# A graph network on one core: at most two row gathers in flight, counted by two alternating semaphores

## The chip, the cores and the metric

The kernel runs on one core of one Trainium2 chip. The metric is the device time in microseconds (us) of one launch, the median of several runs. TensorE multiplies matrices, VectorE and ScalarE do elementwise work, GpSimd issues the gathers (DMAs that fetch rows by a list of indices), SyncE issues the plain loads and stores.

## The reference

Four graph layers over the same 206,250 directed edges, sorted by target, and 6,250 nodes of 128 features. Layer 0 is a message network, layers 1 to 3 are attention layers with 4, 4 and 8 heads. Between them stand residual additions and layer norms. Cut to what matters:

```python
# layer 0
msg_in = concatenate([x[src], x[tgt], edge_features], axis=-1)
messages = relu(msg_in @ W1 + b1) @ W2 + b2
agg = segment_sum(messages, tgt, num_segments=n) / counts
# layers 1 to 3, with small differences
h = (x @ W).reshape(n, HEADS, C)
e = leaky_relu(a_s[src] + a_d[dst], NEG_SLOPE)
p = exp(e - segment_max(e, dst)[dst])
out = segment_sum(h[src] * (p / segment_sum(p, dst)[dst])[:, :, None], dst)
```

What counts here is `x[src]` and `h[src]`: for every edge a row of a table in device memory is fetched by the number of the edge's source node.

## The kernel before, in words

The edges are cut into tiles of 128 and chunks of K = 13 tiles; there are CH = 124 chunks, PAIRS = 62 pairs of them. Each layer runs over all the chunks and then does its work on the nodes (a node stage), which writes the table of rows for the next layer. A table row has 128 numbers (512 bytes) in layer 0 and 144 (576 bytes) in layers 1 to 3.

The gathered rows of a chunk stand in `G`, which has two buffers, b = 0 and 1, for even and odd chunks. GpSimd's function `edges` (L562 to L570) waits until the chunk's indices are loaded and, past the first two chunks of a layer, until the messages of the chunk before last have been made from the same buffer. It then issues 13 gathers of 128 rows each, with no wait between them. All 13 count on one semaphore `gathered[l][b]`, of which there is one for each layer and buffer; a DMA adds 16 to it when it has landed. So 4 x 124 x 13 = 6448 gathers are issued, in order, from one queue.

Who waits for `gathered`: SyncE at L436 ahead of loading the indices two chunks on (behind it are queued the loads of edge features in layer 0 and of marks and joins in the others); ScalarE at L980 in layers 1 to 3 ahead of its copy of the source scores out of `G` (the copy helper's line is L925); VectorE at L1272 in layer 0 ahead of the four additions at L1276. The messages of a chunk are ready after L1276 and L1281 in layer 0, and after the multiplication at L1356 in the others. TensorE turns the membership tiles (L703), multiplies and adds up the messages by target (L713), and does the small products of the attention. Work on chunk c+1 is interleaved with that on chunk c by an order written out by hand on each engine.

Of the kernel before, what the change touches and what calls it, by code (L numbers as in the profile page):

```python
# [5 lines left out]
def gnn_program(nc, A, out):  # L6
# [20 lines left out]
    K = A["src"].shape[2]  # L27
    CH = A["src"].shape[0]
    TILES = K * CH
    PAIRS = CH // 2  # L30
# [26 lines left out]
    with ctx:  # L57
        def sb(name, shape, dt=fp32):
            return ctx.enter_context(nc.sbuf_tensor(name, shape, dt))
# [3 lines left out]
        def sem(name, counter=False):  # L63
            s = ctx.enter_context(nc.semaphore(name))
            if counter:
                counters.append(s)
            return s
# [23 lines left out]
        idx = sb("idx", [P, 2, K], i32)  # L91
# [146 lines left out]
        x_loaded = [sem(f"features_loaded{k}") for k in range(4)]  # L238
        row0_stored = [sem(f"first_rows_stored{k}") for k in range(4)]
        gather_paced = sem("gather_paced")  # L240
        built = sem("constants_built")
        cleared = sem("weights_cleared")
        targets_in = sem("targets_loaded")
# [8 lines left out]
        adz_clear = sem("padded_scores_cleared")  # L252


        gathered = [[sem(f"gathered_l{l}_{b}") for b in range(2)] for l in range(4)]
        idx_loaded = [sem(f"indices_loaded{b}") for b in range(2)]
        ef_loaded = [sem(f"edge_features_loaded{b}") for b in range(2)]
        marks_loaded = [sem(f"marks_loaded{b}") for b in range(2)]
# [87 lines left out]
        def past(l, c):  # L346

            return 2 + CH * l + c

        def gpast(l, c):  # L350

            return 2 + CH * (l - 1) + c
# [3 lines left out]
        def _(sp):  # L356
# [15 lines left out]
            def load_indices(l, c, b):  # L372
                sp.dma_start(idx[:, b, :], A["src"][bass.ds(c, 1), :, :]
                             .rearrange("o p k -> p (o k)")).then_inc(idx_loaded[b], 16)

            def load_edge_features(c, b):
                t0 = c * (K * P)
                sp.dma_start(ef[0:ED, b, :], A["edge_attr_64"][:, bass.ds(t0, EF)]).then_inc(ef_loaded[b], 16)
                sp.dma_start(ef[ED:2 * ED, b, 0:K * P - EF],
                             A["edge_attr_64"][:, bass.ds(t0 + EF, K * P - EF)]).then_inc(ef_loaded[b], 16)  # L380
# [47 lines left out]
            def load_marks(l, c, b):  # L428
                sp.dma_start(marks[0:JH, b, :], marks_all[bass.ds(c * K, K), :].unsqueeze(0)
                             .to_broadcast([H, K, 3 * P])).then_inc(marks_loaded[b], 16)  # L430
                sp.dma_start(join[0:1, b, :], joins_all[bass.ds(c, 1), :]).then_inc(marks_loaded[b], 16)

            def edges(l, c, b, h, last=False):
                if last:
                    return
                sp.wait_ge(gathered[l][b], 16 * K * (h + 1))  # L436
                load_indices(l, c + 2, b)
                if l == 0:
                    sp.wait_ge(pre_ready[3], past(0, c))
                    load_edge_features(c + 2, b)  # L440
                else:
                    sp.wait_ge(max_ready, gpast(l, c))
                    sp.wait_ge(maxf_ready, gpast(l, c))
                    sp.wait_ge(carry_ready, gpast(l, c))
                    load_marks(l, c + 2, b)
# [73 lines left out]
            for s in range(NS):  # L519
                left = min(BLK, N - s * BLK)  # L520
                sp.wait_ge(n_xnew, OUTER + s + 1)
                r = (INNER + s) % 3
# [11 lines left out]
        def _(pool):  # L534
# [27 lines left out]
            def edges(l, c, b, h, early=False):  # L562
                pool.wait_ge(idx_loaded[b], 16 * (PAIRS * l + h + 1))
                if not early:
                    pool.wait_ge(messages, past(l, c - 2))
                pool.sem_inc(gather_paced, 1)
                for t in range(K):
                    nc.gpsimd.indirect_dma_start(  # L568
                        G[:, b, t, 0:rows[l].shape[1]], None, rows[l],
                        bass.IndirectOffsetOnAxis(idx[:, b, t:t + 1], 0)).then_inc(gathered[l][b], 16)  # L570

            def base_rows(l, s):

# [349 lines left out]
        def _(act):  # L923
            def copy(dst, src):
                return nc.scalar.activation(dst, src, ACT.Copy)  # L925
# [18 lines left out]
            def keep_turned(l, c, j):  # L944
                act.wait_ge(turned[j], past(l, c))
                if l == 0:
                    act.wait_ge(pre_ready[j], past(l, c - 1))
                k0, k1 = BATCH[j]
                copy(membT[:, k0:k1, :], ps_mT[j % 2][:, 0:(k1 - k0) * P].rearrange("p (k n) -> p k n", k=k1 - k0)
                     ).then_inc(turned_kept[j], 1)  # L950
# [26 lines left out]
                        keep_turned(0, c + 1, j)  # L977

            def attention(l, c, b, h, ahead=True):
                act.wait_ge(gathered[l][b], 16 * K * (h + 1))  # L980
                copy(sflat[:, :].rearrange("p (h k) -> p h k", h=H),
                     G[:, b, :, MW:SW].rearrange("p k h -> p h k")).then_inc(sc_kept, 1)
                if ahead:
                    pad_scores(l, c + 1)
                act.wait_ge(seg_fwd, gpast(l, c))
                copy(pair_sm[0:JH, 0:P], ps_sc[b][0:JH, :]).then_inc(sc_copied, 1)
                if ahead:
                    keep_turned(l, c + 1, 0)
                    keep_turned(l, c + 1, 1)
                act.wait_ge(fac_diff, gpast(l, c))  # L990
                nc.scalar.activation(factor[0:1, 2 * H:3 * H], factor[0:1, 2 * H:3 * H], ACT.Exp).then_inc(fac_exp, 1)
                if ahead:
                    keep_turned(l, c + 1, 2)
                if l == 1:
                    act.wait_ge(maxf_turned, gpast(l, c))
                    copy(msg[:, b, :, MW:SW].rearrange("p k h -> p h k"),
                         ps_max.rearrange("p (h k) -> p h k", h=H)).then_inc(maxf_kept, 1)
                act.wait_ge(diff_ready, gpast(l, c))
                nc.scalar.activation(wgt[0:JH, :], diff[0:JH, :], ACT.Exp).then_inc(wgt_ready, 1)  # L999
                if ahead:  # L1000
                    keep_turned(l, c + 1, 3)
# [142 lines left out]
        def _(dve):  # L1144
# [120 lines left out]
            def mlp(c, b, h, prev=True, ahead=True):  # L1265
                if ahead:
                    make_membership(0, c + 1, 1 - b)
                if prev:
                    win = window_numbers(c - 1)
                    dve.wait_ge(summed[2], past(0, c - 1))  # L1270
                    add_sums(0, c - 1, win, 0, GR)
                dve.wait_ge(gathered[0][b], 16 * K * (h + 1))  # L1272
                for j in range(4):
                    k0, k1 = BATCH[j]
                    dve.wait_ge(pre_ready[j], past(0, c))
                    o = tt(msg[:, b, k0:k1, 0:P], G[:, b, k0:k1, 0:P],  # L1276
                           ps_pre[j % 2][:, 0:(k1 - k0) * P].rearrange("p (k f) -> p k f", k=k1 - k0),
                           ALU.add)
                    o.then_inc(pre_added[j], 1)
                dve.wait_ge(pre_added[3], past(0, c))  # L1280
                dve.sem_inc(messages, 1)  # L1281
# [429 lines left out]
```

## Time and profile before

| | before |
|---|---|
| median of 3 runs | 8751.18 us (8750.0 to 8758.39) |
| span of the profiled execution | 12335.1 us |
| TensorE clock granted in it, share of full speed | 0.727 |
| TensorE busy | 7368.8 us |
| GpSimd busy | 6252.3 us |
| VectorE busy | 5183.6 us |
| ScalarE busy | 2180.5 us |
| chunks, gathers | 496, 6448 |

The profiled execution is much longer than the timed ones. So the profile's durations of single instructions and distances between them can be used, and its idle times only with care. In the rows a line of the timeline gives the start in us from the span's start, the duration in us, the engine, the line of the kernel, the operation, output and inputs, how many instructions the row holds, and in square brackets how long the engine had been idle and what ended that.

### The profile page before, as it was taken

The numbers are of one execution on the slowest core, as the hardware profiler recorded it, in microseconds if no ns is written. First come the engines' busy times: TensorE is split into PE (matmuls) and PEld (weight loads), VectorE is DVE, ScalarE is ACT, GpSimd is POOL, SyncE is SP. The second block draws the span as 40 slices with busy tenths as digits, with TensorE's granted clock in tenths as the row PEclk, the third lists the DMA queues.
The fourth block names the chain that finished last, engine by engine and source line by source line (L and its number), as shares of the span: only waits on it lengthen the run. The fifth ranks groups of instructions, "written<-read, shape, count | busy, mean of one in ns | idle before, by whom it ended". The sixth has DMA issues, their size and how long they took to land.

```text
span 12335.1 us, 141293 instructions
## 1 busy us (share of the span) xinstructions
PE 7368.8 (60%) x41611; PEld 6500.9 (53%) x41612; DVE 5183.6 (42%) x13628; ACT 2180.5 (18%) x7255; POOL 6252.3 (51%) x6594
## 2 busy tenths in 40 slices
PE   5666666666565555665565555555555555565554
PEld 5655555555555545554455555554544555555554
DVE  3222222224444444444464444444445444444445
ACT  2111111112111111111121111111112111111112
POOL 4555555554455545554445555555544555555553
PEclk7777777777777777777767777777776777777776
DMA  3222222222211111111122121121112221111111
GB/s 88 55 55 55 55 54 55 56 55 59 51 47 47 47 45 47 47 46 45 46 67 48 47 48 48 48 48 48 47 47 55 49 48 48 48 48 48 48 48 42
DMA packets 425594, 625.69 MB, mean 51 GB/s; under 512 B 189754, under 2 KB 305737, under 8 KB 425285
## 3 DMA queue, kind: packets, MB, share of 16 engines
q0 software_dynamic: 206336, 462.61, 15.4%
q1 hardware_dynamic: 218910, 160.84, 5.0%
q10 hardware_dynamic: 296, 1.65, 0.0%
q8 instruction: 20, 0.33, 0.0%
q14 instruction: 32, 0.26, 0.0%
HBM read 598.03 MB, written 26.58 MB: 51 GB/s over the span
## 4 chain that ended last, share of the span: by engine, by line
another core or an unknown queue 29%; PE 25%; DVE 23%; issue 16%; DVEq 4%; ACT 2%; POOL 1%; DMA 0%; SPq 0%; ACTq 0%; POOLq 0%
PE ps L713 12%; PE ps L760 7%; DVE acc L1263 5%; DVE memb L1183 4%; DVEq L1237 2%; PE ps L703 2%; DVE msg L1356 2%; DVE msg L1276 1%; DVEq L1263 1%; PE ps L791 1%; DVE acc L1253 1%; DVE shared L1310 1%; PE ps L795 1%; DVE shared L1348 1%
## 5 line engine op out<-in xcount | busy, mean ns | idle before, releaser
L568 POOL DMA_INDIRECT G<-rows,idx x6448 | 6112.1, 948 | 5686.5 <-DVE msg L1356 2881.2
L713 PE MATMUL ps<-msg,memb 128*128 128x136 f32 (+2 forms) x12896 | 2052.4, 328 | 62.9 <-DVE msg L1356 62.2
L760 PE MATMUL ps<-membT,shared 128*104 128x128 f32 x9672 | 2082.8, 400 | 2.2 <-ACT membT L925 2.2
L713 PEld LDWEIGHTS ps<-msg,memb 128*128 128x128 f32 x12896 | 1976.0, 236 | 84.0 <-issue 41.1
L760 PEld LDWEIGHTS ps<-membT,shared 128*104 128x104 f32 x9672 | 1874.9, 270 | 29.5 <-issue 3.0
L703 PE MATMUL ps<-ident,memb 128*128 128x128 f32 x6448 | 1108.2, 302 | 1137.5 <-issue 750.3
L1183 DVE TENSOR_TENSOR memb<-rel,ps 128x768 f32<-128x768 f32 x1488 | 1044.4, 729 | 1509.1 <-PE ps L713 1227.7
L703 PEld LDWEIGHTS ps<-ident,memb 128*128 128x128 f32 x6448 | 770.4, 150 | 1393.4 <-issue 1034.4
L925 ACT ACTIVATE membT<-ps 128x512 f32<-128x512 f32 x1984 | 991.3, 510 | 1961.8 <-remote 1639.2
L732 PE MATMUL ps<-shared,membT 128*128 x3224 | 813.8, 336 | 754.2 <-DVE msg L1276 472.5
L1263 DVE TENSOR_TENSOR acc<-acc,ps 128x136 f32 (+2 forms) x3472 | 1023.0, 295 | 561.7 <-issue 315.5
L732 PEld LDWEIGHTS ps<-shared,membT 128*128 128x128 f32 x3224 | 624.2, 237 | 830.5 <-issue 829.8
L781 PE MATMUL ps<-ones,shared 1*104 1x1 f32 x1488 | 284.7, 291 | 1288.1 <-issue 778.7
L781 PEld LDWEIGHTS ps<-ones,shared 1*104 1x104 f32 x1488 | 263.7, 259 | 1363.8 <-issue 825.9
L1276 DVE TENSOR_TENSOR msg<-G,ps 128x512 f32<-128x512 f32 x496 | 288.0, 587 | 1519.0 <-remote 1174.2
L735 PE MATMUL ps<-w1e,shared 128*128 128x128 f32 x3224 | 787.1, 328 | 89.0 <-issue 82.4
L1356 DVE TENSOR_TENSOR msg<-G,ps 128x1768 f32<-128x1768 f32 x372 | 742.4, 1996 | 110.7 <-PE ps L791 96.8
L1310 DVE TENSOR_TENSOR_SCAN shared<-shared,ps 1x112 f32<-1x112 f32 x372 | 139.2, 374 | 1381.9 <-remote 1298.1
L1337 DVE SCALAR_TENSOR_TENSOR shared<-shared,ps 104x128 f32<-104x128 f32 x372 | 132.4, 356 | 1385.7 <-remote 1311.1
L735 PEld LDWEIGHTS ps<-w1e,shared 128*128 128x128 f32 x3224 | 630.2, 239 | 122.3 <-issue 122.0
L968 ACT ACTIVATE msg<-msg 128x512 f32<-128x512 f32 x496 | 272.4, 549 | 2388.8 <-DVE msg L1276 1953.9
L791 PE MATMUL ps<-ident,shared 104*128 104x104 f32 x372 | 141.3, 380 | 882.8 <-ACT shared L999 741.1
(182 smaller groups left out, 4864.9 us busy)
## 6 DMA issues: line engine op xcount, KB each, us to landing
G<-rows,idx POOLq DMA_INDIRECT x6448
shared<-marks_all SPq DMA_DIRECT2D x372, 156.0 KB
shared<-in_edge_attr SPq DMA_DIRECT2D x124, 256.0 KB
shared<-in_edge_attr SPq DMA_DIRECT2D x124, 160.0 KB
rows<-msg SPq DMA_DIRECT2D x36, 288.0 KB, 2.7
idx<-in_src SPq DMA_DIRECT2D x496, 6.5 KB
xrows<-msg SPq DMA_DIRECT2D x24, 256.0 KB, 2.2
memb<-xrows SPq DMA_DIRECT2D x24, 256.0 KB, 2.9
```

The costliest lines, as they stand in the source:

```text
L568: nc.gpsimd.indirect_dma_start(G[:, b, t, 0:rows[l].shape[1]], None, rows[l], bass.IndirectOffsetOnAxis(idx[:, b, t:t + 1], 0)).then_inc(g ...
L703: last = nc.tensor.transpose(ps_mT[j % 2][:, o:o + P], memb[:, b, k * P:(k + 1) * P], ident[:, :])
L713: last = mm(ps_sum[k // 2][:, 0:width], memb[:, b, k * P:(k + 1) * P], msg[:, b, k, 0:width], start=k % 2 == 0, stop=k % 2 == 1 or k == K - 1)
L732: mm(o, membT[:, k, :], btab[:, bass.ds(win[k // 2], 1), :].rearrange("p o f -> p (o f)"), start=True, stop=False)
L735: last = mm(o, ef[:, b, (k - h * HALF) * P:(k - h * HALF + 1) * P], w1e[:, h, :], start=False, stop=True)
L760: last = mm(ps_sc[b][0:JH, :], adz[:, k // 2, K - 1 - k:K - 1 - k + JH], membT[:, k, :], start=k == 0, stop=False)
L781: last = mm(ps_col[0:JH, w:w + 1], carry[0:1, w * JH:(w + 1) * JH], ones[0:1, 0:1], start=True, stop=True)
L925: return nc.scalar.activation(dst, src, ACT.Copy)
L1183: last = tt(memb[:, b, k0 * P:k1 * P].rearrange("p (k n) -> p k n", k=n), r, w, ALU.is_equal)
L1263: tt(a, a, ps_sum[g][:, 0:width], ALU.add).then_inc(added[g], 1)
L1276: o = tt(msg[:, b, k0:k1, 0:P], G[:, b, k0:k1, 0:P], ps_pre[j % 2][:, 0:(k1 - k0) * P].rearrange("p (k f) -> p k f", k=k1 - k0), ALU.add)
L1356: tt(msg[:, b, :, 0:MW].rearrange("p k (h f) -> p k h f", h=H), G[:, b, :, 0:MW].rearrange("p k (h f) -> p k h f", h=H), ps_wgt.rearrange( ...
```

## The change

The gathers of a chunk count on two semaphores in turn, `gathered[b][r]` with r = t % 2 for tile t, one pair for each buffer, used in all four layers (the layers' numbers are in the target values). Ahead of gather t, for t of 2 and more, GpSimd waits until the gather of tile t-2 has landed, and increments `gather_paced`, a counter that nobody waits for. Everyone who waited for `gathered[l][b]` waits for both semaphores of the buffer.

```diff
+        indices_paced = sem("indices_paced")
-        gathered = [[sem(f"gathered_l{l}_{b}") for b in range(2)] for l in range(4)]
+        IN_FLIGHT = 2
+        TURNS = [len(range(r, K, IN_FLIGHT)) for r in range(IN_FLIGHT)]
+        gathered = [[sem(f"rows_gathered{b}_{r}") for r in range(IN_FLIGHT)] for b in range(2)]
...
-                sp.wait_ge(gathered[l][b], 16 * K * (h + 1))
+                for r in range(IN_FLIGHT):
+                    if r:
+                        sp.sem_inc(indices_paced, 1)
+                    sp.wait_ge(gathered[b][r], 16 * TURNS[r] * (PAIRS * l + h + 1))
...
                 for t in range(K):
+                    r, before = t % IN_FLIGHT, t // IN_FLIGHT
+                    if before:
+                        pool.wait_ge(gathered[b][r], 16 * (TURNS[r] * (PAIRS * l + h) + before))
+                        pool.sem_inc(gather_paced, 1)
                     nc.gpsimd.indirect_dma_start(
                         G[:, b, t, 0:rows[l].shape[1]], None, rows[l],
-                        bass.IndirectOffsetOnAxis(idx[:, b, t:t + 1], 0)).then_inc(gathered[l][b], 16)
+                        bass.IndirectOffsetOnAxis(idx[:, b, t:t + 1], 0)).then_inc(gathered[b][r], 16)
...
-                act.wait_ge(gathered[l][b], 16 * K * (h + 1))
+                for r in range(IN_FLIGHT):
+                    act.wait_ge(gathered[b][r], 16 * TURNS[r] * (PAIRS * l + h + 1))
...
-                dve.wait_ge(gathered[0][b], 16 * K * (h + 1))
+                for r in range(IN_FLIGHT):
+                    dve.wait_ge(gathered[b][r], 16 * TURNS[r] * (h + 1))
```

## Rows read from the trace of the kernel before

**Rows 1.** The page: span, busy time, the chain that ended last, the gathers.

```profile
span 12335.1 us, 141293 instructions
PE 7368.8 (60%) x41611; PEld 6500.9 (53%) x41612; DVE 5183.6 (42%) x13628; ACT 2180.5 (18%) x7255; POOL 6252.3 (51%) x6594
another core or an unknown queue 29%; PE 25%; DVE 23%; issue 16%; DVEq 4%; ACT 2%; POOL 1%; DMA 0%; SPq 0%; ACTq 0%; POOLq 0%
...
L568 POOL DMA_INDIRECT G<-rows,idx x6448 | 6112.1, 948 | 5686.5 <-DVE msg L1356 2881.2
```

**Rows 2.** The chain by time, in layer 2: start, us, what.

```profile
8013.32 4.33 another core or an unknown queue
...
8036.94 8.59 another core or an unknown queue
```

**Rows 3.** The timeline of GpSimd, a chunk of layer 0 and its next.

```profile
1501.64 0.94 POOL L568 DMA_INDIRECT G<-rows,idx  x1 [7.55 <-DVEq L1281]
1502.88 0.94 POOL L568 DMA_INDIRECT G<-rows,idx  x1 [0.30 <-issue]
...
1516.62 0.95 POOL L568 DMA_INDIRECT G<-rows,idx  x1 [0.30 <-issue]
1525.09 0.94 POOL L568 DMA_INDIRECT G<-rows,idx  x1 [7.53 <-DVEq L1281]
```

**Rows 4.** The same view, first and last gathers of the layers, in order.

```profile
33.86 1.43 POOL L568 DMA_INDIRECT G<-rows,idx  x1 [30.16 <-DMA rows<-msg]
...
92.89 0.94 POOL L568 DMA_INDIRECT G<-rows,idx  x1 [22.75 <-DVEq L1281]
...
2946.54 0.94 POOL L568 DMA_INDIRECT G<-rows,idx  x1 [0.30 <-issue]
3100.67 1.02 POOL L568 DMA_INDIRECT G<-rows,idx  x1 [8.66 <-DMA rows<-msg]
...
6106.53 0.94 POOL L568 DMA_INDIRECT G<-rows,idx  x1 [0.30 <-issue]
6284.75 1.04 POOL L568 DMA_INDIRECT G<-rows,idx  x1 [8.63 <-DMA rows<-msg]
...
9203.58 0.95 POOL L568 DMA_INDIRECT G<-rows,idx  x1 [0.30 <-issue]
9318.92 1.02 POOL L568 DMA_INDIRECT G<-rows,idx  x1 [8.18 <-DMA rows<-msg]
...
12220.74 0.94 POOL L568 DMA_INDIRECT G<-rows,idx  x1 [0.30 <-issue]
```

**Rows 5.** The timeline in layer 2: messages made, first gather of the next chunk.

```profile
8000.74 2.00 DVE L1356 TENSOR_TENSOR msg<-G,ps 128x1768 f32<-128x1768 f32 x1
8003.52 0.94 POOL L568 DMA_INDIRECT G<-rows,idx  x1 [7.75 <-DVE msg L1356]
```

**Rows 6.** DMA queues: packets, MB, busy share of the 16 engines.

```profile
q0 software_dynamic: 206336, 462.61, 15.4%
```

**Rows 7.** The timeline at two layers' starts: the 13th gather, ScalarE's first copy.

```profile
3115.73 0.95 POOL L568 DMA_INDIRECT G<-rows,idx  x1 [0.30 <-issue]
3118.26 0.38 ACT L925 ACTIVATE shared<-G 128x104 f32<-128x104 f32 x1 [12.70 <-DMA G<-rows,idx]
...
6299.84 0.94 POOL L568 DMA_INDIRECT G<-rows,idx  x1 [0.30 <-issue]
6302.46 0.38 ACT L925 ACTIVATE shared<-G 128x104 f32<-128x104 f32 x1 [12.79 <-DMA G<-rows,idx]
```

**Rows 8.** DMA issues by line: count, KB each, median us to landing.

```profile
shared<-marks_all SPq DMA_DIRECT2D x372, 156.0 KB
shared<-in_edge_attr SPq DMA_DIRECT2D x124, 256.0 KB
shared<-in_edge_attr SPq DMA_DIRECT2D x124, 160.0 KB
...
xT<-in_x_cols SPq DMA_DIRECT2D x1, 768.0 KB, 7.1
```

## The prediction

> **What bounds the kernel now.** I first set the profiled execution beside the timed runs. Its span is 12,335 us, the median of the runs is 8,751 us, so the profile is 41% too long and its waits can't be read as the waits of a timed run. The chain that ended last says where the excess sits: 29% of it is "another core or an unknown queue" [rows 1], and 12,335 x (1 - 0.29) = 8,758 us, the median almost to the microsecond. In the chunk loops these are holes of 4 to 9 us in which VectorE waits for something the profile doesn't show, although its visible producers are done [rows 2]. I take them for a burden of the profiled execution and ask what is left.
>
> Next the GpSimd timeline. Inside a chunk the 13 gathers start 1.248 us apart, a record of 0.94 and a gap of 0.30, always the same: in layer 0 from 1501.64 to 1516.62 is 12 steps [rows 3]. So 13 x 1.248 = 16.22 us of GpSimd for each chunk, and 496 x 16.22 = 8,047 us in all for the 6448 gathers. The time outside: 33.9 us before the first gather and 23.7 - 1.25 = 22.4 us in which gather 27 waits for the set-up; from the start of each layer's last gather to the next layer's first 154, 178 and 115 us, and 114 from the last one to the end, less the 1.25 that each last gather has itself: 557 us [rows 1, 4]. Together 34 + 22 + 8,047 + 557 = 8,660 us, 91 us (1%) under the median. Two sums that have nothing to do with each other land at the timed value. I read it so: in a timed run GpSimd issues gathers back to back for nearly all of each layer, and the rest of the work (TensorE, VectorE) needs about as long, 16.2 to 16.4 us per chunk, just behind it. In the profiled execution GpSimd idles 7.5 to 7.8 us ahead of every chunk, waiting for the messages of the chunk before last [rows 3, 5]; that slack belongs to the holes. Bandwidth is no limit: the gathers' queue has the 16 DMA engines busy 15.4% [rows 6].
>
> **The change, part by part.** (1) Gather t of a chunk, for t = 2 to 12, is now behind a wait until gather t-2 of the same chunk has landed, and one semaphore instruction. That is 11 x 496 = 5,456 added waits on the queue that sets the time. What is queued behind each: all later gathers, in layers 1 to 3 of the next chunk too. Who waits for that: VectorE (layer 0) or ScalarE (layers 1 to 3), and SyncE, which loads the indices of the chunk after next once the last gather has landed.
>
> The trace before has no such wait, so I build its price from two rows. Landing: at the start of layers 1 to 3 ScalarE sits idle for the first 13 gathers and copies from G when the last has landed. Start of gather 13 to start of the copy is 3118.26 - 3115.73 = 2.53 and 6302.46 - 6299.84 = 2.62 in layers 1 and 2; I take 2.57 us [rows 7]. Release: the first gather of a chunk follows exactly the pair of instructions that is now put before the others (wait, semaphore increment). VectorE's multiplication ends at 8000.74 + 2.00 = 8002.74, the gather starts at 8003.52: 0.78 us [rows 5]. So a gather that waits for the last but one starts 2.57 + 0.78 = 3.35 us after that one, and two gathers come every 3.35 us in place of every 2.50. Where the record puts a gather's start drops out of the sum.
>
> A chunk then needs: gathers 0, 2, ..., 12 are six steps of 3.35 = 20.10 us, and the next chunk's first gather follows 1.25 later (its wait is for the other buffer and has been met). 21.35 us against 16.22, plus 5.13 us. Times 496 chunks: 2,544 us. In layer 0 the first two chunks' longer issue lies in the 22.4 us that gather 27 waited for the set-up, so 2 x 5.1 = 10 us come back. Sum: 8,751 + 2,534 = 11,285 us.
>
> Bounds of the pair's 3.35 us. From below: the landing can't be missing, and at the least the 0.30 gap between two records stays, so 2.53 + 0.30 = 2.83 us; 6 x 2.83 + 1.25 = 18.23 us a chunk, plus 2.01 x 496 = 997, 9,750 us. This would be so if most of the 0.78 is a start from rest, or if the profiler lengthens both. A gain is excluded, as gathers can't come closer than 1.248 us and the chunk already stands at 13 of them. From above: the landings were read with no other traffic. In layer 0 SyncE loads 416 KB per chunk, in the others 156 KB; a load of 768 KB took 7.1 us to land, about 9.5 us per MB, so 4 and 1.5 us, and a gather caught behind one lands that much later [rows 8]. If that came in full once a chunk: 124 x 4 + 372 x 1.5 = 1,054 us; I count half, 530, up to 11,800. I take 3.35, since the rows are of the same two steps that are added, and nothing in them looks like a hole.
>
> (2) Four semaphores for gathers in place of eight; the counts run on over the layers. No cost. (3) ScalarE, VectorE and SyncE wait for two semaphores in place of one. The second is met at about the same moment; each is 0.1 us or less of sequencer work, 372 times on ScalarE and 124 on VectorE, on engines that idle more than half of the time [rows 1]. On SyncE the index load, the edge features and the marks are queued behind it; it waits for VectorE most of the time and their buffers are not wanted for a chunk. Nothing. Without that cover it would be some 50 us. (4) What else becomes later: landing of chunk c+2 comes 0.78 + 20.10 + 2.57 = 23.5 us after the messages of c, in place of 18.3; up to its own messages there are two periods, 42.7 us, so 19 us remain for a chunk's dependent work, while 16.4 us is the whole of a period now. GpSimd stays the one that sets the pace, and TensorE and VectorE wait some 5 us per chunk.
>
> The Trainium skill speaks against this size. "DMA: Bandwidth & Descriptors", section "Anatomy of one DMA — SWDGE (gpsimd) path", gives about 2.0 us fixed plus the bytes by 436 GB/s for such a DMA. For 128 rows of 512 or 576 bytes an estimate by that page is 2.2 us. By it two in flight would be enough and the change would cost nothing; the landing rows alone (2.57 from the record's start, the release not in them) are already longer [rows 7].
>
> **The rivals.** *The pair takes 2.50 us or less in a timed run.* Then the wait is met as the sequencer comes to it and nothing is lost, 8,750 us; this is also what one would see if the change didn't hold gathers back. For it: the profiled execution is slower in so much else. Against: two landings agree within 0.1 us, in stretches with no hole. It is what the skill's formula above would give.
>
> *The slack is real.* GpSimd idles 7.5 us per chunk in the profile [rows 3, 5]; 5.13 more would vanish in it. It needs a timed run whose 16.4 us per chunk belong to TensorE and VectorE, and gathers that go faster unprofiled: with a step of 0.94 (the bare record) and a pair of 2.57 (the bare landing) 6 x 2.57 + 0.94 = 16.4 us, so 8,750 to 8,800. For it: TensorE is busy 7,369 us, 14.9 per chunk, nearly as much as GpSimd [rows 1]. Against: needs both bare values at once. It would explain an unchanged *profiled* span, 23.5 us being more than 21.35, and I expect just that.
>
> *Release costs only the gap.* 9,750 us, worked out above, and what lies between it and the sum.
>
> *Faster.* The unknown holes come from many gathers in flight (a descriptor ring that fills), and some of them are left in timed runs; with two in flight they vanish. The chunk can still not go under 13 x 1.248 = 16.22 us, so at most the 91 us between sum and median: 8,660 us. It decides only if the pair is under 2.50. Against it: a full ring would show in the gathers' own records, and these are 0.94 us in the middle of a layer, with a mean of 948 ns over all 6448 [rows 1, 3].
>
> **How the numbers follow.** Forecast 11,285 us (a pair of 3.1 to 3.5 us with or without traffic, 10,500 to 11,800): 0.62. Between 9,750 and 10,500: 0.20. Above 11,800: 0.05. The two rivals without loss: 0.09 together. Faster: 0.02. A slowdown smaller than 1,000 us: 0.02. The range from 9,750 to 11,800 leaves out 0.18. A measurement of this kernel tells about 0.2% (18 us) from no change: faster by more 0.02, within 0.09, slower by more 0.89.
>
> **What would show it.** In the profile after, the gathers of a chunk should come in pairs, starts alternating 1.25 and about 2.1 us apart, gather 12 about 20 us after gather 0, with GpSimd idle ahead of every second one for DMA. Its idle time for VectorE's messages should fall from 7.5 to 2.5 us a chunk, and the profiled span move far less than the median. Landing after the start, 2.57: if it is 2.0, I am wrong towards no change. Starts 1.42 apart on average would be the lower bound. A loss much smaller than 496 x 6 x what the pair has grown would say that GpSimd had slack in the timed run. Holes that are gone from the chain, and a median below 8,750, would be the last rival.

## The result, and the profile after

The changed kernel takes 11,456.2 us (11,451.9 to 11,461.5, 4 runs), the kernel before 8,754.1 us beside it: a ratio of 1.3086, 95% interval 1.3067 to 1.3104, or 2,702 us lost. 11,285 had been forecast.

One thing has to be said before any number of an experiment. The kernel before doesn't take the same time wherever and whenever it is run: beside the experiments below it took 8,753 and 8,757 us on two occasions and 12,346, 12,770 and 12,886 us on three others, within 0.7% in each, and the same chip gave 12,346 once and 8,757 later. The changed kernel took 11,456 beside a before of 8,754 and 11,442 beside one of 12,886. So every ratio below belongs to the time of the kernel before beside it, which the tables give; I call them the short condition (8,75x) and the long one (over 12,000). The profiled execution shown ahead of the prediction, with its 12,335 us, is one of the long condition; the median beside it, 8,751 us, is of the short one. A lower clock isn't what tells the conditions apart: TensorE's granted clock was 0.719 in the changed kernel's profile of either one.

The page after, the lines that answer to [rows 1] and [rows 6]:

```profile
span 11456.1 us, 150895 instructions
PE 7219.9 (63%) x41611; PEld 6422.2 (56%) x41612; DVE 5154.7 (45%) x13628; ACT 2035.7 (18%) x7255; POOL 6257.4 (55%) x6594
...
q0 software_dynamic: 206336, 462.61, 16.8%
...
DMA 65%; issue 25%; POOL 6%; POOLq 1%; DVE 1%; PE 0%; ACT 0%; DVEq 0%; SPq 0%; ACTq 0%
DMA G<-rows,idx 65%; POOL G L578 5%; POOLq L576 1%; POOLq L577 0%; POOL rstd L618 0%; DMA rows<-msg 0%; POOL membT L608 0%; POOLq L649 0%; POOLq L571 0%; PE ps L723 0%; DVE acc L1427 0%; DVE acc L1426 0%; DVE stats L1401 0%; POOL memb L590 
...
L578 POOL DMA_INDIRECT G<-rows,idx x6448 | 6116.6, 949 | 4833.6 <-DMA G<-rows,idx 3468.9
```

Busy times are those of before. What is new is the idle time ahead of the gathers (L578, which was L568): 3,469 us of it end with a gather's landing, and the chain that ended last is gathers, one waiting for another, from end to end. "Another core or an unknown queue" is gone from it, 29% before. This profile's span is the median itself, so here the trace can be read as a timed run. Its chain in layer 2, by time (start, us, what):

```profile
8003.57 2.52 DMA G<-rows,idx
8006.10 0.02 issue
8006.12 0.02 POOLq L577
8006.14 0.52 issue
8006.66 0.04 POOLq L576
8006.69 0.18 issue
8006.87 0.56 POOL G L578
...
8008.17 3.12 DMA G<-rows,idx
...
8012.07 2.59 DMA G<-rows,idx
```

A gather lands 2.52 us after its start, then 0.78 us pass (the wait L576 and the increment L577 among them) until the gather it held back starts: 3.30 us. The one from 8008.17 needs 3.12 + 0.78 = 3.90. The timeline of the same stretch, GpSimd and SyncE's queue:

```profile
8003.57 0.94 POOL L578 DMA_INDIRECT G<-rows,idx  x1 [1.57 <-DMA G<-rows,idx]
8004.82 0.94 POOL L578 DMA_INDIRECT G<-rows,idx  x1 [0.30 <-issue]
8006.87 0.94 POOL L578 DMA_INDIRECT G<-rows,idx  x1 [1.11 <-DMA G<-rows,idx]
...
8007.91 0.73 SPq L432 DMA_DIRECT2D shared<-marks_all  x1
...
8008.17 0.94 POOL L578 DMA_INDIRECT G<-rows,idx  x1 [0.35 <-issue]
...
8008.85 0.26 SPq L434 DMA_DIRECT2D shared<-joins_all  x1
...
8010.28 0.94 POOL L578 DMA_INDIRECT G<-rows,idx  x1 [1.17 <-DMA G<-rows,idx]
8012.07 0.94 POOL L578 DMA_INDIRECT G<-rows,idx  x1 [0.85 <-DMA G<-rows,idx]
```

Gathers come in pairs, 1.25 and some 2.05 us apart; the one that lands late was issued 0.26 us after SyncE's load of 156 KB of marks (L432). Over all chunks, from the start of gather t-2 to that of gather t: median 3.34 us, mean 3.49, 4.38 at the 95th percentile. The late ones sit beside SyncE's loads in the whole trace: where no load of marks or edge features is issued within 3 us of the start of gather t-2 (3,893 cases) the median is 3.33 us; where a load of marks is issued within 0.25 us of it (213 cases) it is 4.04; and where a load of edge features, 256 or 160 KB, is issued from 0.75 us before it to 1.25 us after it (211 cases) it is 4.45. First to last gather of a chunk 20.6 to 20.75 us in the four layers, and from chunk to chunk 22.01, 21.87, 21.97 and 21.96 us (124 chunks each, less a layer's first two). The first and the last gathers of the layers, as in [rows 4]:

```profile
33.79 1.47 POOL L578 DMA_INDIRECT G<-rows,idx  x1 [30.09 <-DMA rows<-msg]
...
2773.90 0.94 POOL L578 DMA_INDIRECT G<-rows,idx  x1 [1.02 <-DMA G<-rows,idx]
...
2918.65 1.02 POOL L578 DMA_INDIRECT G<-rows,idx  x1 [7.59 <-DMA rows<-msg]
...
5629.19 0.94 POOL L578 DMA_INDIRECT G<-rows,idx  x1 [1.14 <-DMA G<-rows,idx]
```

Outside the chunks stand 33.8 us at the start, then 144.8, 170.1 and 108.4 between the layers and 106.2 at the end, 563 us together; the rest is 496 x 21.95 = 10,887, in all 11,450 of 11,456.

### The profile page after: what moved, and what is told of

Its sections match the earlier page's. It is cut to its first block, busy times and chain, and to the rows that moved or that the text cites. A ratio compares the mean times of both kernels' runs of the same rounds, so it can differ in the third digit from the quotient of the medians.

```text
span 11456.1 us, 150895 instructions
## 1 busy us (share of the span) xinstructions
PE 7219.9 (63%) x41611; PEld 6422.2 (56%) x41612; DVE 5154.7 (45%) x13628; ACT 2035.7 (18%) x7255; POOL 6257.4 (55%) x6594
## 4 chain that ended last, share of the span: by engine, by line
DMA 65%; issue 25%; POOL 6%; POOLq 1%; DVE 1%; PE 0%; ACT 0%; DVEq 0%; SPq 0%; ACTq 0%
DMA G<-rows,idx 65%; POOL G L578 5%; POOLq L576 1%; POOLq L577 0%; POOL rstd L618 0%; DMA rows<-msg 0%; POOL membT L608 0%; POOLq L649 0%; POOLq L571 0%; PE ps L723 0%; DVE acc L1427 0%; DVE acc L1426 0%; DVE stats L1401 0%; POOL memb L590 0%; POOL memb L595 0%
## 5 line engine op out<-in xcount | busy, mean ns | idle before, releaser
L578 POOL DMA_INDIRECT G<-rows,idx x6448 | 6116.6, 949 | 4833.6 <-DMA G<-rows,idx 3468.9
L770 PE MATMUL ps<-membT,shared 128*104 128x128 f32 x9672 | 1950.7, 383 | 2.2 <-ACT membT L935 2.2
L770 PEld LDWEIGHTS ps<-membT,shared 128*104 128x104 f32 x9672 | 1799.4, 260 | 19.1 <-issue 3.0
L723 PE MATMUL ps<-msg,memb 128*128 128x136 f32 (+2 forms) x12896 | 1687.3, 289 | 133.8 <-DVE msg L1368 132.5
L723 PEld LDWEIGHTS ps<-msg,memb 128*128 128x128 f32 x12896 | 1602.7, 197 | 161.9 <-DVE msg L1368 82.2
L777 PE MATMUL ps<-ident,shared 128*104 128x128 f32 x744 | 268.6, 462 | 2042.0 <-ACT shared L935 2042.0
L713 PE MATMUL ps<-ident,memb 128*128 128x128 f32 x6448 | 1443.8, 387 | 27.0 <-issue 16.3
L777 PEld LDWEIGHTS ps<-ident,shared 128*104 128x104 f32 x744 | 149.3, 259 | 2118.8 <-ACT shared L935 2118.8
L713 PEld LDWEIGHTS ps<-ident,memb 128*128 128x128 f32 x6448 | 1179.4, 205 | 160.0 <-issue 135.7
L1306 DVE TENSOR_TENSOR_SCAN shared<-shared,ps 104x128 f32<-104x128 f32 x372 | 156.6, 421 | 2008.1 <-PE ps L777 2008.1
L935 ACT ACTIVATE shared<-G 128x104 f32<-128x104 f32 x372 | 139.6, 375 | 4306.4 <-DMA G<-rows,idx 4306.4
```

What stands on the lines that cost most here:

```text
L578: nc.gpsimd.indirect_dma_start(G[:, b, t, 0:rows[l].shape[1]], None, rows[l], bass.IndirectOffsetOnAxis(idx[:, b, t:t + 1], 0)).then_inc(g ...
L713: last = nc.tensor.transpose(ps_mT[j % 2][:, o:o + P], memb[:, b, k * P:(k + 1) * P], ident[:, :])
L723: last = mm(ps_sum[k // 2][:, 0:width], memb[:, b, k * P:(k + 1) * P], msg[:, b, k, 0:width], start=k % 2 == 0, stop=k % 2 == 1 or k == K - 1)
L770: last = mm(ps_sc[b][0:JH, :], adz[:, k // 2, K - 1 - k:K - 1 - k + JH], membT[:, k, :], start=k == 0, stop=False)
L777: mm(ps_sc[b][0:JH, :], sflat[:, :], ident[:, :], start=False, stop=True).then_inc(sc_ready, 1)
```

## The experiments

All times are medians in us; "beside" is the kernel before, timed on the same chip together with the variant.

| kernel | time | beside | ratio, 95% interval |
|---|---|---|---|
| split_unpaced | 12,323.8 | 12,346.3 | 0.9988 (0.9972 to 1.0003) |
| one_in_flight | 21,300.3 | 12,346.3 | 1.7245 (1.7203 to 1.7287) |
| three_in_flight | 12,626.5 | 12,346.3 | 1.0218 (1.0195 to 1.0242) |
| twelve_gathers | 11,732.8 | 12,346.3 | 0.9498 (0.9474 to 0.9523) |
| two_in_flight_again | 11,441.7 | 12,886.4 | 0.8878 (0.8863 to 0.8894) |
| short_op_between | 11,852.5 | 12,770.0 | 0.9286 (0.9260 to 0.9312) |
| long_op_between | 11,885.4 | 12,770.0 | 0.9307 (0.9284 to 0.9330) |
| one_pause | 11,930.0 | 12,770.0 | 0.9342 (0.9319 to 0.9365) |
| no_gathers | 7,918.1 | 8,752.9 | 0.9047 (0.9031 to 0.9062) |
| busy_without_dma | 8,922.6 | 8,752.9 | 1.0193 (1.0176 to 1.0210) |
| narrow_gathers | 8,750.8 | 8,752.9 | 0.9994 (0.9985 to 1.0004) |
| three_narrow | 8,887.1 | 8,757.2 | 1.0148 (1.0131 to 1.0164) |

### Is it the wait, and is it the pair of 3.35 us?

**split_unpaced**: the changed kernel with the semaphores split, but nothing held back.

```diff
-                    if before:
-                        pool.wait_ge(gathered[b][r], 16 * (TURNS[r] * (PAIRS * l + h) + before))
-                        pool.sem_inc(gather_paced, 1)
```

> The changed kernel without the wait and the increment on GpSimd: two semaphores in turn for each buffer, everyone else waits for both, and gathers are issued back to back as before. Theory: the split costs nothing, 8,754 us, within 0.3%. Rival (the doubled waits on ScalarE, VectorE and SyncE are a part of the loss): up to 100 us more.

Measured 0.9988, no difference: two semaphores, and two waits in place of one on ScalarE, VectorE and SyncE, cost nothing. This was in the long condition, where GpSimd has idle time, but the added waits aren't on GpSimd.

**one_in_flight**: the kernel before, each gather behind the landing of the last.

```diff
                 for t in range(K):
+                    if t:
+                        pool.wait_ge(gathered[l][b], 16 * (K * h + t))
+                        pool.sem_inc(gather_paced, 1)
```

> The kernel before, with its own semaphores, in which every gather but the first of a chunk waits until the one before it has landed. Theory: every step is release plus landing, 3.34 us, and in one step per chunk about 0.9 more behind a load. Chunk 12 x 3.34 + 0.9 + 1.25 = 42.2 us; 496 x 42.2 + 563 outside the chunks + 22 at the start = 21,500 us, and not less than 20,800. Rival (landing is shorter when fewer are in flight, say 2.0 for 2.5): 12 x 2.8 + 1.25 = 34.9, 17,900 us.

21,300 us against 21,500. The timeline of GpSimd in layer 1:

```profile
8003.81 0.94 POOL L571 DMA_INDIRECT G<-rows,idx  x1 [2.33 <-DMA G<-rows,idx]
8007.14 0.94 POOL L571 DMA_INDIRECT G<-rows,idx  x1 [2.39 <-DMA G<-rows,idx]
8010.48 0.94 POOL L571 DMA_INDIRECT G<-rows,idx  x1 [2.40 <-DMA G<-rows,idx]
8013.77 0.94 POOL L571 DMA_INDIRECT G<-rows,idx  x1 [2.35 <-DMA G<-rows,idx]
```

Steps of 3.29 to 3.34 us (the layers' medians are 3.28 to 3.33), with one gather in the air and nothing else to delay it: landing and release together don't depend on whether one or two are in flight. The longest step of a chunk has a median of 3.4 us in layer 0 and of 4.0 in the others, where it stands beside SyncE's load of marks; a chunk takes 41.2 to 42.1 us.

**three_in_flight**: `IN_FLIGHT = 3` in the changed kernel.

> The changed kernel with three semaphores in turn: gather t waits for gather t-3 in place of t-2. Nothing else differs, so there are 10 x 496 = 4,960 waits and increments on GpSimd in place of 5,456. Theory (the loss is the time a gather has to wait for the landing): a waiting gather starts 3.34 us after the one it waits for (the median in the changed kernel's trace), and three steps of 1.248 are 3.74 us, so the wait has been met; only a gather that lands about 1 us late behind a load of SyncE's costs some 0.5 us in a chunk. 8,750 to 9,000 us. Rival (the added instructions themselves cost, some 0.5 us each): 10/11 of the loss stays, 11,200 us.

12,627 us, far from what was expected, since it was run in the long condition. It still says that the waits are met as a rule: the median step is 1.25 us, first to last gather of a chunk takes 15.2 to 15.5 us on the layers' averages in place of 15.0, and GpSimd waits for the messages of the chunk before last as it did before. The chain and the gathers' group:

```profile
another core or an unknown queue 30%; PE 27%; DVE 20%; issue 16%; DVEq 4%; ACT 1%; POOL 1%; DMA 0%; SPq 0%; ACTq 0%; POOLq 0%
...
L578 POOL DMA_INDIRECT G<-rows,idx x6448 | 6115.5, 948 | 5984.6 <-DVE msg L1368 3128.3
```

The holes of [rows 2] are there with three in flight and gone with two.

**three_narrow**: the same, with narrow rows past a layer's first two chunks, in the short condition.

```diff
-        IN_FLIGHT = 2
+        IN_FLIGHT = 3
...
+                wide = rows[l].shape[1] if early else 16
+                table = rows[l] if early else rows[l].rearrange("n (q c) -> (n q) c", c=16)
...
-                        G[:, b, t, 0:rows[l].shape[1]], None, rows[l],
+                        G[:, b, t, 0:wide], None, table,
```

> The changed kernel with three gathers in flight in place of two, and, past a layer's first two chunks, each gather reads rows of 64 bytes in place of 512 or 576 (part of the output is therefore not computed; row width alone moved nothing where the kernel before takes 8,753 us). What it can tell depends on what the kernel before takes beside it. (a) Before takes about 8,753 us (no holes): three gathers back to back cover 3.75 us, more than the 3.34 from a gather's start through its landing and the release, so every wait is met as GpSimd comes to it, and the time should be within 0.5% of the kernel before, 8,710 to 8,800. If the wait itself costs on GpSimd's queue even when it is met, by 0.05 us or more each, 4,960 waits give at least 9,000. (b) Before takes over 12,000 us (holes in which VectorE and ScalarE wait for TensorE): theory 'the holes come from how closely the gathers are issued': they stay with narrow rows, 12,000 to 12,900 us, as three in flight gave 12,627 with wide rows. Rival 'the holes come from the bytes that the gathers move into the on-chip memory': with an eighth of the bytes they vanish, 8,750 to 9,500.

8,887 us, above the 8,710 to 8,800 expected and under the 9,000 of a wait that always costs. Two pieces of its timeline in layer 2:

```profile
5019.71 0.94 POOL L580 DMA_INDIRECT G<-rows,idx  x1 [0.30 <-DMA G<-rows,idx]
5020.95 0.94 POOL L580 DMA_INDIRECT G<-rows,idx  x1 [0.30 <-DMA G<-rows,idx]
...
5023.27 0.72 SPq L432 DMA_DIRECT2D shared<-marks_all  x1
...
5023.45 0.95 POOL L580 DMA_INDIRECT G<-rows,idx  x1 [0.30 <-DMA G<-rows,idx]
...
5024.20 0.27 SPq L434 DMA_DIRECT2D shared<-joins_all  x1
...
5025.96 0.95 POOL L580 DMA_INDIRECT G<-rows,idx  x1 [0.30 <-issue]
5027.62 0.94 POOL L580 DMA_INDIRECT G<-rows,idx  x1 [0.71 <-DMA G<-rows,idx]
```

The usual wait is met: steps of 1.25, gap 0.30. But the gather of 5023.45, issued 0.18 us after the marks' load, holds back the third after it until 5027.62, 4.17 us later in place of 3.34 or less, and three in flight cover only 3 x 1.25 = 3.75. GpSimd's idle time ahead of the gathers is 2,255.6 us here and 2,120.8 in narrow_gathers (below), 135 more; the spans differ by 8,885.3 - 8,748.8 = 137 us. So landings that SyncE's loads delay account for the price of three in flight; a met wait that cost 0.05 us would have made it 248 us. By layer the chunk is 17.12, 16.77, 16.56 and 16.56 us, in narrow_gathers 16.31, 17.01, 16.30 and 16.30: some 100 us are lost in layer 0, where edge features are loaded, 32 in each of layers 2 and 3, and layer 1 gains 30.

### Does GpSimd set the pace in the short condition?

**no_gathers**: past a layer's first two chunks each chunk's 13 gathers are one small addition on GpSimd, and those who wait for the rows wait for that.

```diff
-                for t in range(K):
-                    nc.gpsimd.indirect_dma_start(
+                for t in range(K if early else 1):
+                    if early:
+                        nc.gpsimd.indirect_dma_start(
...
+                    else:
+                        nc.gpsimd.tensor_tensor(filler[:, b, t, :], ones[:, 0:4], ones[:, 0:4], ALU.add).then_inc(filled[b], 1)
```

> The kernel before in which GpSimd, past the first two chunks of a layer, issues no gather but one addition of 4 columns per chunk; everyone else does the full work on the rows of the first two chunks. It gives the floor that TensorE, VectorE and ScalarE set with GpSimd out of the way. Theory (at 8,754 us GpSimd's 16.2 us per chunk was the limit and the others came just behind): a chunk of 14 to 16 us, so 7,500 to 8,500 us, and no holes in the chain, wherever it runs. Rival 1 (the others set 16.4 us by themselves): 8,700 us or more. Rival 2 (the holes have nothing to do with gathers): 12,000 us where the kernel before takes 12,350 or more.

**busy_without_dma**: the same with 13 powers of 6 columns in place of the one addition, which keep GpSimd busy as the gathers do, without a DMA.

```diff
+                for t in range(K if early else 13):
...
+                        nc.gpsimd.tensor_tensor(filler[:, b, t, :], ones[:, 0:6], ones[:, 0:6], ALU.pow).then_inc(filled[b], 1)
```

> The same, but GpSimd computes 13 powers of 6 columns per chunk (0.57 us for one column and 0.98 for four in the profile of before, so some 1.25 each) in place of the 13 gathers: as busy as with gathers, and no DMA. A chunk of 16.3 to 17 us by GpSimd. Theory A (the holes come from the gathers' DMA traffic or their descriptors): no holes, 8,700 to 9,100 us anywhere. Theory B (they come from GpSimd being busy without a pause): holes stay, near the time of the kernel before.

**narrow_gathers**: all the gathers, but rows of 64 bytes (the edit of three_narrow, one set of semaphores, nothing held back).

> The kernel before in which the gathers past the first two chunks of a layer fetch rows of 16 numbers (64 bytes) in place of 128 or 144, by the same indices: as many GpSimd instructions and rows, an eighth of the bytes. If the holes come from the bytes that the gathers write: few holes, well under the kernel before, down to 8,750 us. If they come from the number of rows, descriptors or completions: within 3% of the kernel before.

Without gathers 7,918 us, so the other engines' work is 835 us shorter than the kernel before; per chunk (7,918 - 563) / 496 = 14.8 us (TensorE's granted clock was 0.86 in it and 0.82 in narrow_gathers, so 14.8 may be a little too few). The average hides a layer: a chunk takes 11.9 us in layer 0, 17.0 in layer 1 and 15.1 in layers 2 and 3. Four chunks of layer 1:

```profile
1755.90 0.20 POOL L578 TENSOR_TENSOR filler<-ones 128x4 f32<-128x4 f32 x1 [16.65 <-DVE msg L1368]
...
1824.26 0.20 POOL L578 TENSOR_TENSOR filler<-ones 128x4 f32<-128x4 f32 x1 [16.64 <-DVE msg L1368]
```

So in layer 1 the other engines need more than the 16.22 us of GpSimd's gathers; in the other three layers they need less.

With GpSimd computing thirteen powers a chunk, 1.29 us apart (their records are 1.317 long and overlap), it is 8,923 us, inside the 8,700 to 9,100 expected, and the chain says "POOL 63%". With an eighth or a ninth of the bytes of a row (the same indices then also reach only into a smaller part of the table) it is 8,751, no difference. This last trace is one of a kernel of 8,750 us, which the prediction didn't have; its chain and its gathers:

```profile
POOL 41%; issue 24%; PE 18%; DVE 12%; DMA 3%; DVEq 3%; ACT 1%; POOLq 0%; SPq 0%; ACTq 0%
...
L570 POOL DMA_INDIRECT G<-rows,idx x6448 | 6121.6, 949 | 2120.8 <-issue 1934.3
...
4999.85 0.94 POOL L570 DMA_INDIRECT G<-rows,idx  x1 [0.30 <-DVE msg L1358]
5001.10 0.95 POOL L570 DMA_INDIRECT G<-rows,idx  x1 [0.30 <-issue]
...
5014.90 0.94 POOL L570 DMA_INDIRECT G<-rows,idx  x1 [0.30 <-issue]
5016.14 0.94 POOL L570 DMA_INDIRECT G<-rows,idx  x1 [0.30 <-DVE msg L1358]
```

No hole in it. The gathers run back to back over the chunks' borders too, layer 1 apart: the messages are ready as the 13th gather has been issued, and the wait of 7.5 us of [rows 3, 5] isn't there. The chunks take 16.31, 17.01, 16.30 and 16.30 us in layers 0 to 3, 16.48 on average, in place of 13 x 1.248 = 16.22. Layer 1's 17.01 is what it needs without gathers, at the same granted clock of 0.80.

### What are the holes of the long condition?

**two_in_flight_again**: the changed kernel itself once more.

> The changed kernel once more, because the kernel before was timed at 8,754 us in one place and at 12,346 us beside the runs with three, one and split semaphores. The 12,335 us of its profiled execution was therefore no burden of the profiler. Where the kernel before takes 8,750 us: theory and rival both say 11,456 us. Where it takes 12,350 us: theory (the holes come with gathers back to back; two in flight leave none, and the time is GpSimd's wait for landings in either place) 11,456 us, that is 7% under the kernel before. Rival (the holes belong to the place and lie on top of whatever the kernel does): above 12,350 us, up to 15,000.

It fell beside a before of 12,886 us and took 11,442, 11% less. No wait in its trace ends with an unknown releaser.

**twelve_gathers**: the 13th gather of a chunk is left out past a layer's first two chunks.

```diff
-                for t in range(K):
+                for t in range(K if early else MOST):
```

> The kernel before without the 13th gather of each chunk past the first two of a layer (the last tile then works on the rows of an earlier chunk; all other work is done). 488 gathers fewer. Theory (GpSimd issues back to back and sets the time): 488 x 1.248 = 609 us less, 8,145 us. Rival (TensorE and VectorE set the 16.4 us of a chunk and GpSimd has slack in timed runs): no change, 8,754 us. In between: what of the 609 us is missing says how close behind the others are.

613 us less for 488 gathers fewer, 1.257 us each (609 us expected): the step of 1.248 comes back in full, though GpSimd idles 7.6 us ahead of a chunk (the median) in this trace. So in the long condition too the length of the burst of gathers goes into the time in full, through something other than GpSimd being busy.

**short_op_between** and **long_op_between**: ahead of each gather but a chunk's first, GpSimd does one small operation, an addition of 4 columns or a power of one.

```diff
+                    if t:
+                        for j in range(1):
+                            nc.gpsimd.tensor_tensor(filler[:, b, t, j, :], ones[:, 0:4], ones[:, 0:4], ALU.add).then_inc(filled, 1)
```

> The kernel before with a small GpSimd addition of 4 columns (some 0.2 us) ahead of each gather but the first of a chunk; no wait for a landing. The step grows from 1.25 to some 1.45 us, GpSimd's own time for a chunk to 18.7 us, the whole by GpSimd alone to 563 + 22 + 496 x 18.7 = 9,860 us. Theory (the holes of the places where the kernel before takes 12,350 or more come from gathers issued with no pause): fewer holes or none, between 9,860 and 11,000 us there. Rival (what counts is that no more than two are in flight; a landing takes 2.55 us, so with steps of 1.45 there are two as a rule): 9,860 too, and the same kernel with a longer step must be without holes. Second rival (the holes have nothing to do with the pace): 12,350 or more. In a place without holes: 9,860 us.

> The same with a power of one column (0.57 us in the profile of before) ahead of each gather but the first. Steps of some 1.85 us, a chunk 23.4 us, by GpSimd alone 12,200 us in any place; no holes in the chain by the theory, whatever the place, as the landing (2.55 us) leaves fewer than two in flight and GpSimd is the one that sets the pace. Rival (a landing has to be waited for, the pace is not enough): holes stay, 13,500 us or more where the kernel before has them.

**one_pause**: one pause in the middle of the burst, five powers ahead of the 8th gather.

```diff
+                    if t == 7:
+                        for j in range(5):
+                            nc.gpsimd.tensor_tensor(filler[:, b, t, j, :], ones[:, 0:4], ones[:, 0:4], ALU.pow).then_inc(filled, 1)
```

> The kernel before with one pause of some 5 us (five powers of 4 columns, 0.98 us each) ahead of the 8th gather of a chunk; within the two halves gathers follow each other every 1.25 us. Mean pace as in the changed kernel, a chunk 21.2 us by GpSimd alone, 11,100 us in all. Theory A (holes come when three gathers overlap, as they do with steps of 1.25): holes stay, since the steps are what they were; more than 12,000 us where the kernel before takes 12,350. Theory B (holes come when GpSimd has been busy for long on end, or are simply the time that a chunk's work waits for GpSimd's burst to end): most are gone, 11,100 to 11,500 us. In a place without holes: 11,100 us.

All three are 6.6 to 7.1% faster than the kernel before beside them, though each gives GpSimd more to do. Against what was expected: the addition makes the step 1.35 us and not 1.45, and 11,852 lies above the 9,860 to 11,000 that few holes would give; the power makes it 1.78 and not 1.85, which is why 11,885 lies under 12,200; and 11,930 with one pause lies between the two theories' times. With steps of 1.35 us the holes stay, 22% of the chain; with steps of 1.78 not one is left and the chain is "POOL 74%". In one_pause they stay, 29% of the chain.

Who waits in the holes can be read in the trace before, where waits whose end the profile puts down to no instruction are called "remote" (who, total us, times, longest us):

```profile
ACT membT L925 <- remote: 1639.2, 570, 5.6
DVE shared L1310 <- remote: 1298.1, 308, 15.4
```

With two more groups of VectorE, at L1337 (1,311 us) and L1276 (1,174 us), they are nearly all; each of the four waits for a semaphore that TensorE increments. The timeline of one_pause:

```profile
8018.47 0.94 POOL L576 DMA_INDIRECT G<-rows,idx  x1 [0.30 <-issue]
...
8019.38 0.85 PE L780 MATMUL ps<-ident,shared 104*1 104x104 f32 x4 [1.59 <-DVE shared L1308]
...
8019.72 0.94 POOL L576 DMA_INDIRECT G<-rows,idx  x1 [0.30 <-issue]
...
8020.97 0.94 POOL L576 DMA_INDIRECT G<-rows,idx  x1 [0.30 <-issue]
...
8022.22 0.94 POOL L576 DMA_INDIRECT G<-rows,idx  x1 [0.30 <-issue]
8023.18 3.99 POOL L575 TENSOR_TENSOR filler<-ones 128x4 f32<-128x4 f32 x4
8025.63 1.08 ACT L933 ACTIVATE membT<-ps 128x512 f32<-128x512 f32 x2 [6.59 <-remote]
8025.78 0.38 DVE L1318 TENSOR_TENSOR_SCAN shared<-shared,ps 1x112 f32<-1x112 f32 x1 [4.77 <-remote]
```

ScalarE and VectorE both wait for products of TensorE; those that VectorE wants at 8025.78 are recorded from 8019.38 on. Both waits end 3.4 to 3.6 us after the last gather of the half was issued, that is 0.8 to 1.0 after it has landed by the 2.57 of [rows 7], while the pause still goes on. That is one common place and not the only one. Of the 529 waits of this kind over 3 us in this trace 155 end while gathers are still being issued closely, 146 within 2.6 us of the last start and 227 from 2.6 to 3.9 us after it, and 1 ends later; in the trace before it is 397, 93, 411 and 4 of 905. So hardly a hole outlasts a burst by more than 3.9 us. It is the close succession of gathers that goes with them: GpSimd's load alone doesn't bring them (long_op_between has more of it and no hole), nor does the mean pace over a chunk (1.67 us a gather in one_pause with holes, 1.72 in the changed kernel without).

## Why the prediction came out as it did

The forecast was 11,285 us, in a range of 9,750 to 11,800; 11,456 were measured, 171 more. Step by step:

**GpSimd sets the pace, 16.22 us a chunk: right in three layers of four.** narrow_gathers shows the gathers back to back at 1.25 us, and no_gathers that nothing else would need 8,754. The others are not "just behind it", though: by no_gathers they need 11.9 us a chunk in layer 0 and 15.1 in layers 2 and 3. In layer 1 they need 17.0 and set the pace themselves before the change. Against the 21.35 us of a chunk after it this makes no difference to the forecast.

**The step of a pair, 3.35 us: right.** Median 3.34 over all pairs, 2.52 landing and 0.78 release in the chain, and 3.29 to 3.34 with a single one in flight. The rival "2.50 or less" fell with it, and so did "release costs only the gap", which needed 2.83. The estimate of 2.2 us from the Trainium skill ("DMA: Bandwidth & Descriptors", section "Anatomy of one DMA — SWDGE (gpsimd) path") is under the bare landing of 2.52 here, and by it two in flight would have been enough; the measurement decides.

**Late landings: the term that was mis-sized.** The forecast's chunk was 6 x 3.35 + 1.25 = 21.35 us, with none of them in it; the prediction knew of them only as its upper end (4 or 1.5 us a chunk, half counted in the range). Measured are 21.95 us, and the mean pair of 3.49 beside a median of 3.34 says why: 0.60 us a chunk, some 298 us in all, in the gathers issued beside SyncE's loads. The upper end had 4 us for it in layer 0 and 1.5 in the others; the chunk is 0.66 us longer than 21.35 in layer 0 and 0.52 to 0.62 in the others. three_narrow isolates it: with the usual wait met, late landings alone cost 135 us. That the load is the cause is read from where late landings stand in the traces (3.33 us away from loads, 4.04 and 4.45 beside them); moving a load wasn't tried.

**The rest that the sum couldn't place, 91 us, and the time outside the chunks.** The forecast started from the median and so carried these along as if they lay outside the chunks. narrow_gathers has them inside: chunks of 16.48 in place of 16.22, 496 x 0.26 = 129 us, most of it in layer 1 with 17.01, where the other engines set the pace. At 21.95 us a chunk the messages are never late (the trace after has no idle time of GpSimd for them), and the time is gone. Outside the chunks are 563 us after, where the prediction has 34 + 22 + 557 + 91 - 10 = 694. Of these 131 us 91 are the unplaced ones and 33 come from the stretches at the layers' ends, which are 144.8, 170.1, 108.4 and 106.2 us here, 525 less the last gathers' own time: the 557 had been read in a trace of the long condition. Seven are left open. So 298 - 131 = 167 of the 171 us. That the sum came within 1.5% is in part luck, since the two errors have opposite signs; with the late landings alone it would have missed by 298, still inside the range.

**Edits (2) and (3) at nothing: right**, split_unpaced.

**The holes as a burden of the profiled execution: wrong.** That 12,335 x 0.71 is 8,758, close to the median, was a coincidence, or at best says that without the holes the two conditions are alike. The holes are in timed runs too, of the long condition: the timed medians there are 12,346 to 12,886. This step fell without hurting the number, because the median to be predicted was one of the short condition, where they are missing. What hung on it fell too. I expected the slack of 7.5 us ahead of a chunk to swallow most of the change in the profiled span, 12,335 to about the same; it became 11,456, since holes and slack vanished together. And the rival "faster" was capped at 91 us. Its mechanism, holes from many gathers in flight that go away with two, is just what happens in the long condition, and there it is worth 11%, 1,445 us beside 12,886. My argument against it, that a full ring would show in the gathers' own records, rules out no more than that one cause: the records stay at 0.94 us and TensorE's results are what comes late.

**What stays open.** Why closely issued gathers hold up TensorE's results, and what makes a place or a time one of the long condition. With a landing of 2.57 us the step fixes how many gathers are in flight on average (2.1 at 1.25 us, 1.9 at 1.35, 1.4 at 1.78, 1.5 at the changed kernel's 20.7 / 12 = 1.7), so number and spacing can't be told apart by these runs. Whether the holes depend on the bytes wasn't seen: both narrow kernels fell into the short condition. Which of the two kernels is the better one depends on the condition: before at 8,754 against 11,456 in the one, 12,346 to 12,886 against 11,442 in the other. No version beat both kernels in both: three in flight is at 1.015 (with narrow rows) and 1.022, and the ones with an operation in between, 11,850 to 11,930, were run in the long condition only, where they lose to two in flight.

## What to carry to other kernels

If an engine issues DMAs back to back and sets the pace, each wait for a landing costs what landing plus release are longer than the issues that cover them: n x 1.25 against 3.34 us here, so one in flight costs 2.1 us a gather, two cost 0.42 and three nothing but the late ones (1.5% here, with narrow rows). Read landing and release from the trace before, from the same two steps elsewhere in the kernel, and add a term for the landings that another queue's loads delay, since a wait turns each of them into lost time. And where a profile's span and the timed median differ by 40%, don't put it down to the profiler unasked: here the profile was of another condition of the machine, which timed runs met too. Last, look at the pace by layer before you call one engine the limit: an average of 14.8 us a chunk hid a layer of 17.0.

## What the runs showed of the hardware

The pace of gathers of 128 rows, 1.248 us each, doesn't depend on the rows' width: the median step is 1.249 us with 64 bytes a row and with 512 to 576. A gather lands 2.52 to 2.57 us after its start, and the next one behind its landing starts 0.78 us later; together it is 3.3 us with one in flight as with two.

One and the same kernel took 8,75x us at some times and 12,3xx to 12,9xx at others. In the second condition VectorE and ScalarE wait, up to 15 us at a time, for semaphores that TensorE increments, and nearly all waits over 3 us end within a burst of gathers or at most 3.9 us after its last one was issued. Gathers 1.7 us apart on average (the changed kernel) or 1.78 (long_op_between) leave no such waits, 1.25 and 1.35 do, and the changed kernel takes the same time in both conditions (11,456 and 11,442 us).

A gather that is issued within 0.25 us of a load of 156 KB on SyncE's queue lands some 0.7 us late (4.04 against 3.33 us to the start of the gather behind it), and one beside a load of 256 or 160 KB some 1.1 us late (4.45), at the median.
